# The 64-tap filter of a delta-rule layer as one triangular token block per channel, with new hand-written engine orders

## The reference, cut to what matters

```python
def _dwconv(x, w):                       # w: one filter of K taps for each channel
    K = w.shape[1]
    xt = jnp.pad(jnp.transpose(x, (0, 2, 1)), ((0, 0), (0, 0), (K - 1, 0)))
    y = jax.lax.conv_general_dilated(xt, w[:, None, :], (1,), 'VALID', ..., feature_group_count=w.shape[0])
    return jnp.transpose(y, (0, 2, 1))
...
v = jax.nn.silu(_dwconv(hs @ Wv, conv_v))
o_d, _ = _delta_rule_chunkwise(bh(q), bh(k), bh(v), jnp.transpose(beta, (0, 2, 1)))
paths = jnp.stack([_dwconv(v, fir_s), _dwconv(v, fir_m), _dwconv(v, fir_l), delta_path, v], axis=3)
```

## Time and profile before

| what | value |
|---|---|
| median of 3 executions | 1418.63 us (1417.29 to 1436.04) |
| span of the profiled execution | 1418.5 us |
| TensorE busy | 1334.8 us, 94% |
| weight loads busy | 1166.4 us, 82% |
| DVE busy | 991.1 us, 70% |
| ACT busy | 682.2 us, 48% |
| fill matmuls (L589) | 1024 records, 134.9 us busy |
| filter matmuls (L2337) | 2624 records, 108.6 us busy |
| delta products (L2210) | 3072 records, 103.1 us busy |

### The profile page before, as it was taken

One profiled execution on the slowest core, in us unless ns is written; L12 is line 12 of the kernel. 1 busy time (PEld: TensorE's weight loads), 2 busy tenths in 40 slices (PEclk: granted clock), 3 DMA queues, 4 the chain that ended last, 5 costly groups with the idle time before them and its releaser, 6 DMA issues.

```text
span 1418.5 us, 42978 instructions
## 1 busy us (share of the span) xinstructions
PE 1334.8 (94%) x18644; PEld 1166.4 (82%) x18644; DVE 991.1 (70%) x2959; ACT 682.2 (48%) x1735; POOL 137.9 (10%) x299
## 2 busy tenths in 40 slices
PE   6999998999986899999999999999999999999997
PEld 6788887888643689899789889788979879989976
DVE  7957898678689554667784567796457778455767
ACT  3535763448377456333447533346632444743332
POOL 3111121111110010100110100011010010010000
PEclk9989999999997899999999999999999999999999
DMA  5000000000230200000000000000000000000001
GB/s 160 2 3 2 3 2 2 3 2 3 77 139 19 77 2 1 2 3 2 2 2 1 2 3 3 1 2 1 1 2 4 2 3 1 1 1 3 3 2 31
DMA packets 8509, 20.33 MB, mean 14 GB/s; under 512 B 2304, under 2 KB 6400, under 8 KB 7808
## 3 DMA queue, kind: packets, MB, share of 16 engines
q1 hardware_dynamic: 8320, 17.58, 3.5%
HBM read 16.53 MB, written 1.05 MB: 12 GB/s over the span
## 4 chain that ended last, share of the span: by engine, by line
PE 47%; DVE 12%; ACT 4%; issue 2%; POOL 1%; DVEq 0%
PE PS L2210 6%; PE PS L2337 6%; PE PS L1935 4%; PE PS L1967 3%; PE PS L1956 3%; PE PS L1922 3%; PE PS L2220 3%; PE PS L589 2%; PE PS L690 2%; ACT AR L1985 2%; PE PS L1947 2%; PE PS L2669 1%; PE PS L2678 1%; PE PS L1819 1%; DVE X L2740 1%
## 5 line engine op out<-in xcount | busy, mean ns | idle before, releaser
L589 PE MATMUL PS<-CC 128*128 128x128 f32 x1024 | 134.9, 279 | 0.0
L589 PEld LDWEIGHTS PS<-CC 128*128 128x128 f32 x1024 | 124.5, 193 | 3.1 <-issue 0.5
L1985 ACT ACTIVATE AR<-PS,SC 128x128 f32<-128x128 f32 x256 | 91.1, 378 | 39.3 <-DVE SC L2013 39.3
L2337 PE MATMUL PS<-AR,PA 64*64 64x256 f32 (+43 forms) x2624 | 108.6, 300 | 0.5 <-issue 0.4
L2210 PEld LDWEIGHTS PS<-AR 64*64 64x64 f32 x3072 | 100.5, 135 | 7.2 <-issue 2.2
L2210 PE MATMUL PS<-AR 64*64 64x32 f32 (+1 forms) x3072 | 103.1, 219 | 0.8 <-DVE AR L2463 0.3
L576 POOL TENSOR_SCALAR SC<-mv 128x2 f32<-128x2 f32 x64 | 13.2, 206 | 837.0 <-DVE mv L562 818.4
L2337 PEld LDWEIGHTS PS<-AR,PA 64*64 64x64 f32 x2624 | 85.0, 133 | 6.9 <-issue 2.7
L2010 DVE TENSOR_REDUCE SC<-PS 128x4 f32<-128x512 f32 x64 | 44.2, 691 | 57.1 <-PE PS L1935 56.7
L1935 PE MATMUL PS<-kvt,AR 128*128 128x128 f32 x512 | 68.8, 279 | 2.6 <-ACT AR L1980 2.6
L1935 PEld LDWEIGHTS PS<-kvt,AR 128*128 128x128 f32 x512 | 63.2, 191 | 7.9 <-ACT AR L1980 6.6
(11 more groups left out here) (552 smaller groups left out, 3334.6 us busy)
## 6 DMA issues: line engine op xcount, KB each, us to landing
WC<-in_cw SPq DMA_DIRECT2D x1, 5438.5 KB, 15.8
PA<-in_fd SPq DMA_DIRECT2D x1, 2624.0 KB, 9.3
PA<-in_stat SPq DMA_DIRECT2D x2, 1280.0 KB, 12.0
X<-in_x SPq DMA_DIRECT2D x2, 512.0 KB, 5.5
...
```

What stands on the lines that cost most here:

```text
L589: T.matmul(bank[int(b)][:, 0:P], lhsT=ident, rhs=CC[:, 0:P], start=True, stop=True)
L1985: A.activation(d.blocks[:, h, :], d.bank[:, h * P:(h + 1) * P], ACT.Exp, scale=D2 ** -0.5, bias=d.most[:, h:h + 1], accum_out=d.total[:, h ...
L2337: m = T.matmul(out_[:, :, first:SEQ], lhsT=FD[rows, tap:tap + 64], rhs=d.vp[rows, :, first + 1 - shift:SEQ + 1 - shift], start=starts, sto ...
```

## The change

The 64-tap filter no longer goes by taps. `v` is brought to PSUM a second time, for each sequence with its tokens on 64 partitions and the channels along the free axis (8 more small matmuls, L2260 of the changed kernel), and one ACT instruction puts it into `vs`. For each channel the 64 taps are stored as one 64x64 triangular block. One matmul per channel multiplies it by that channel's tokens in the four sequences: 64x64 weights by 4 columns. That makes 128 matmuls for a unit (L2359), all with output in c = 1. The 3-tap and 15-tap filters go on by taps, 18 taps by two halves, all with output in c = 0 (L2355). Together there are 164 matmuls as before, in 14 groups. A tap is followed by three or four of the channel matmuls. The stored taps keep their size of 82 blocks. The filters wait for `vs` too.

The way back to token partitions has 8 transposes of 64 partitions (L2371) and 4 matmuls (L2373) instead of 4 transposes and 4 matmuls. ACT copies both short filters in one instruction instead of two.

All turn tables of both parts are new. `FILL_A` has 87 digits instead of 139, `FILL_C` 361 instead of 373. In part C the two streams stand further apart: before, both delta layers of a round ran side by side; now that of stream 0 runs beside the cross attention of stream 1, and that of stream 1 beside the end of stream 0's delta layer and what follows. Apart from fill, filter, the 64 matmuls of L2260 and the way back, the matmuls are the same. In its order TensorE goes 80 times from matmuls of one quarter (L2210, L2337) to other shapes or back before, and 144 times after (L2226, L2260, L2355, L2359).

```diff
-        FILL_A = ("011116666666666666666666666666666666666666666666666666000000000000000002222222111111112133333333"
-            "3333330000000000000000111244441300000000000")
+        FILL_A = ("000133337700000000002222222222222111111544462333333333333300001111112221111111111111111")
...
+                self.vs = ar[:, 768:1024].rearrange("p (q n) -> p q n", q=SQ)
...
 
-        def filter_taps():
-
-
-            one = [(0, s) for s in range(3)] + [(2, s) for s in (0, *range(2, 13), *range(13, 64, 2))]
-            two = [(1, s) for s in range(15)] + [(2, s) for s in (1, *range(14, 64, 2))]
-            assert len(one) == len(two) == 41
-            return list(zip(one, two))
+        NTAPS, FGROUPS = 18, 14
+
+        def filter_products():
+
+
+            products = []
+            for n in range(NTAPS):
+                f, shift = (1, n) if n < 15 else (0, n - 15)
+                for r in range(2):
+                    products.append(("tap", r, f, shift))
+                    done = 2 * n + r
+                    products += [("long", o % 2, o // 2, 0) for o in range(P * done // 36, P * (done + 1) // 36)]
+            assert len(products) == 2 * NTAPS + P
+            return products
 
         def tensor_l3_attention(st):
             k, ps, sc, d = "L3a", st.ps, st.sc, Delta(st)
...
             for j in range(TS):
-                m = T.transpose(ps[:, 3, j * P:(j + 1) * P], d.s3[:, 512 + j * P:512 + (j + 1) * P], ident)
+                T.transpose(ps[:, 3, j * P:(j + 1) * P], d.s3[:, 512 + j * P:512 + (j + 1) * P], ident)
+            for q in range(SQ):
+                for rows in d.halves:
+                    m = T.matmul(ps[rows, 3, ST + q * SEQ:ST + (q + 1) * SEQ],
+                                 lhsT=d.s3[rows, 512 + q * SEQ:512 + (q + 1) * SEQ], rhs=cc("ident64")[rows, :],
+                                 start=True, stop=True)
...
-            taps = filter_taps()
-            for n, pair in enumerate(taps):
-                if n == 0:
-                    T.wait_ge(*a.at(f"{k}.v"))
-                    T.wait_ge(*a.at(f"{k}.local"))
-                    T.wait_ge(fd_there, 16)
-                for c, (f, shift) in enumerate(pair):
-                    K, at = FILTERS[f]
-                    o = 0 if f == 2 else ST
-                    starts = shift == (1 if f == 2 and c else 0)
-                    first = 0 if starts else shift
-                    for r, rows in enumerate(d.halves):
-                        out_ = ps[64 * c:64 * c + 64, r, o:o + ST].rearrange("p (q t) -> p q t", q=SQ)
-                        tap = (at + K - 1 - shift) * 64
-                        m = T.matmul(out_[:, :, first:SEQ], lhsT=FD[rows, tap:tap + 64],
-                                     rhs=d.vp[rows, :, first + 1 - shift:SEQ + 1 - shift], start=starts,
-                                     stop=(shift == K - 1 or (f == 2 and shift == K - 2)))
-                if n % 3 == 2 and n < len(taps) - 2:
+            T.wait_ge(*a.at(f"{k}.v"))
+            T.wait_ge(*a.at(f"{k}.v_seqs"))
+            T.wait_ge(*a.at(f"{k}.local"))
+            T.wait_ge(fd_there, 16)
+            todo = filter_products()
+            for n, (kind, r, what, shift) in enumerate(todo):
+                rows = d.halves[r]
+                if kind == "tap":
+                    K, at = FILTERS[what]
+                    tap = (at + K - 1 - shift) * 64
+                    out_ = ps[0:64, r, what * ST:(what + 1) * ST].rearrange("p (q t) -> p q t", q=SQ)
+                    m = T.matmul(out_[:, :, shift:SEQ], lhsT=FD[rows, tap:tap + 64], rhs=d.vp[rows, :, 1:SEQ + 1 - shift],
+                                 start=(shift == 0), stop=(shift == K - 1))
+                else:
+                    o = (NTAPS + what) * 64
+                    m = T.matmul(ps[64:P, r, SQ * what:SQ * what + SQ], lhsT=FD[rows, o:o + 64], rhs=d.vs[rows, :, what],
+                                 start=True, stop=True)
+                if (n + 1) * FGROUPS // len(todo) > n * FGROUPS // len(todo) and n + 1 < len(todo):
                     yield
             m.then_inc(*p.up(f"{k}.fir"))
             yield
             T.wait_ge(*a.at(f"{k}.fir1"))
-            for j in range(TS):
-                for r in range(2):
-                    o = (2 * j + r) * P
-                    T.transpose(ps[:, 0, o:o + P], d.fir[r][:, ST + j * P:ST + (j + 1) * P], ident)
-                    m = T.matmul(ps[:, 1, o // 2:o // 2 + 64], lhsT=d.fir[r][:, j * P:(j + 1) * P],
-                                 rhs=cc("ident64"), start=True, stop=True)
+            for r in range(2):
+                by_seq = d.fir[r][64:P, 0:ST].rearrange("p (i j g) -> p g j i", j=TS, g=2)
+                for f in range(2):
+                    for j in range(TS):
+                        o = (2 * j + f) * P + 64 * r
+                        T.transpose(ps[:, 0, o:o + 64], d.fir[r][0:64, f * ST + j * P:f * ST + (j + 1) * P], ident[0:64, 0:64])
+                    out_ = ps[64 * f:64 * f + 64, 1, 0:ST].rearrange("p (j r i) -> p r j i", j=TS, r=2)
+                    m = T.matmul(out_[:, r, :, :], lhsT=cc("ident64")[64:P, :], rhs=by_seq[:, f, :, :], start=True, stop=True)
...
             A.wait_ge(*p.at(f"{k}.filtered"))
-            for j in range(TS):
-                A.copy(d.paths[:, j, 0:2, :].rearrange("p f (r n) -> p f r n", r=2),
-                       ps[:, 0, j * ST:(j + 1) * ST].rearrange("p (r f n) -> p f r n", r=2, f=2)).then_inc(*a.up())
+            A.copy(d.paths[:, :, 0:2, :], ps[:, 0, :].rearrange("p (j f n) -> p j f n", j=TS, f=2)).then_inc(*a.up())
             A.copy(d.paths[:, :, 2, :], ps[:, 1, 0:ST].rearrange("p (j n) -> p j n", j=TS)).then_inc(
                 *a.up(f"{k}.filtered"))
...
                          scale=0.5).then_inc(*a.up(f"{k}.path_v"))
+            A.activation(d.vs, ps[:, 3, ST:2 * ST].rearrange("p (q n) -> p q n", q=SQ), ACT.Copy, scale=0.5).then_inc(
+                *a.up(f"{k}.v_seqs"))
...
-    fir = np.concatenate([a3["fir_s"], a3["fir_m"], a3["fir_l"]], axis=1)
-    fd = np.zeros((P, fir.shape[1], 64), np.float32)
-    fd[np.arange(P), :, np.arange(P) % 64] = fir
+    fir = np.concatenate([a3["fir_s"], a3["fir_m"]], axis=1)
+    fd = np.zeros((P, fir.shape[1] + 64, 64), np.float32)
+    fd[np.arange(P), 0:fir.shape[1], np.arange(P) % 64] = fir
+    long = a3["fir_l"].reshape(2, 64, 64)
+    for s_ in range(SEQ):
+        for r in range(2):
+            fd[64 * r + s_, fir.shape[1]:, s_:] = long[r][:, ::-1][:, 0:SEQ - s_]
     path = [0, 1, 2, 4, 3]
```

27 lines of the change are left out of this document (12 added, 15 removed), and 295 rows, old and new, of tables (TURNS_A, TURNS_C).

## The result

The changed kernel takes 1447.18 us (median of 4 executions, 1440.37 to 1456.57), the kernel before on the same chip 1422.45 us. The ratio is 1.0163, with a 95% interval of 1.0107 to 1.0218. I had predicted 1394 us, 1369 to 1425: it is slower, where I expected it faster.

What follows compares the result with a forecast made beforehand. TensorE was taken as the bound where delta products and filters stand. Filters -30, tokens +4, switching +7, way back +3, fill -7 and -2 gave -25 us against 1418.5: 1394 us, range 1369 to 1425.

Steps and rivals of the forecast that it cites:

- The clock of part C: Part C: granted clock noted at 0.99 before, no term in the sum; a lower clock considered only for part A's first 60 us.
- The way back: Transposes and matmuls behind the filters: 1.2 to 2.0 us a unit, 3 us more in all (-2 to 5).
- The filters: L2355 and L2359 in part C: 12.1 to 8.3 us a unit, gain 30 us; L2359 records 23 to 29 ns apart.
- the quarters do not pass each other: Rival at L2355 and L2359: second tap records hold up channel records, 14.6 us a unit; 1445 to 1454 us, chance 0.10.
- The columns' slope: Quarter records in the filters: a floor of 60 ns for few columns, otherwise about 0.85 ns for each column.
- Tokens for the channel matmuls: 8 added matmuls a unit, 16 records in two quarters at 29 ns: 0.5 us, 4 us in all; ACT copy free.
- Switching: Changes between quarters and whole array on TensorE: 64 more at 0.11 us each, 7 us added (2 to 8).
- The fill: Fewer fill matmuls: 52 in part A worth 14 us, half taken as 7 us gain; 12 in part C, 2 us.
- The new turns: New order between delta products: TensorE stays the bound, no net gain or loss, with 15 us either way.
- the delta chain bounds: Rival in part C: chain steps wait longer, TensorE idle passes 60 us; 1418 us (1408 to 1426), chance 0.20.

Runs made afterwards that it cites:

- e8: Changed kernel without 112 of the 128 channel matmuls of each unit, way back still alternating (filter result incomplete); 1440.4 us, ratio 1.011.
- e15: Changed kernel with the way back grouped (all 8 transposes, then the 4 matmuls), a repeat of e5; 1390.8 us, 0.975 of the kernel before.
- e1: Changed kernel with 64 moving columns instead of 4 for each channel matmul; 1466.8 us, 1.028 of the kernel before.
- e16: Changed kernel with the way back grouped and 32 moving columns for each channel matmul; 1396.2 us, 0.978 of the kernel before.
- e4: Changed kernel with the old turn tables and fill in part A alone; 1451.0 us, 1.018 of the kernel before.
- e2: Kernel before, old filters kept, with the changed kernel's turn tables and fill in both parts; 1411.2 us, ratio 0.989.
- e5: Changed kernel with the way back grouped: all 8 transposes first, then the 4 matmuls; 1402.3 us, 0.984 of the kernel before.
- e10: e2 with the changed kernel's alternating way back added as unread work behind its own; 1441.9 us, 1.008 of the kernel before.

## Why the prediction was wrong, point by point

Two steps failed. The clock of part C stood in the sum at nothing, as if it had to stay at 0.99, and cost 60 us. The way back stood in it at 3 us and took 12.5. The first alone turned the gain into a loss, and the second, by its alternation, brought the falls of the clock behind it.

**The filters: right in kind, a little too large.** I said 12.1 to 8.3 us for a unit, -30. With low-clock work counted half, they went from 94.8 to 70.1 us: -25, and 25 ns a record in the first group against the 23 to 29 that I named. The rival "the quarters do not pass each other" had the time almost exactly (1445 to 1454) and is false: the order of time shows them passing, and e8 the taps alone at 7.3 us for a unit beside 8.3 predicted for all. A time that fits proves no mechanism. The "strictly in program order" of the Trainium skill that I cited there does not hold between quarters in these traces: in e15, products that stand behind L2375 in the program start at 605.96, before most of its records. The columns' slope was off: 64 of them are no longer at the floor (e1, 41 ns a record instead of 27), 32 are (e16).

**Tokens for the channel matmuls:** +4 predicted, 4.9 measured (16 records in 0.61 us for a unit).

**Switching: mis-sized, and one kind of change missed.** I took 7 us for 64 changes between quarters and whole array. Products (91.6 to 91.9 us, low-clock work counted half) and the cross attention beside them (146.0 to 147.0) grew by 1 us together. But I had counted the way back's transposes and matmuls as one kind of "other shapes", though they are two. The drain that the cited rule speaks of was there, at seven changes inside each way back.

**The way back: mis-sized.** "At 0.14 and 0.22 without any overlap that is 2.0 us" took prices of the earlier trace rows, where transposes and matmuls had one shape of the array, 128 by 128. It took 3.1 to 3.5 us from start to start, the sum 12.5 us more than before and not 3. The 1.2 to 2.0 us that I named came true in e15, at 1.6 to 1.7.

**The fill:** half of 14 us taken in part A; e4 shows none, within its interval of 0.7% to either side. In the first 60 us TensorE's busy time fell by 10.9 us and the part ended 1 us earlier (its successor begins at 384.8, not 385.9). Less fill became idle time and clock 0.86 instead of 1.00, which the next stretch gave back with 1.00 instead of 0.96. In part C the fill's own time fell by 5 us.

**The new turns:** I took 0, "with 15 us either way". e2 measures 16 us of gain (10 to 23 by its interval, fill included), and the holes of part C shrank from 36 to 17 us. The rival "the delta chain bounds" is refuted: it needed over 60 us idle.

**The clock: the step that was not in the sum.** I wrote that part C had 0.99 and left it there, while the edit took the densest records out of the stretch that is mostly quarter work (2624 filter records of up to 256 columns became 576 of those and 2048 of 4) and put an alternating way back behind them. It cost 60 us. It takes both: the new filters with the grouped way back lost 9 us by the clock in e15 and 27 in e5, the old filters with the alternating one had 59 us at the low clock (e10), which is some 20 us of time over e2 and before. My only sentence on a lower clock was about the first 60 us.

The sum again with what was measured, for part C: -25 (filters) + 5 (tokens) + 1 (switching) + 12.5 (way back) - 5 (fill) - 2 (the rest) - 19 (holes) + 60 (clock) = +27, against 27.3. And for the grouped kernel, e15: -23 + 5 + 5 (switching: products 4, cross attention 1) + 0 - 4 - 2 - 19 (holes) + 9 (clock) = -29, which is the difference of its span of 1389.5 to 1418.5. That this lies near my 1394 is partly luck: the holes, which I had at 0, made up for the clock, which I had left out, and for the fill.

## The better version

The changed kernel with the way back grouped beats both, by the two sets of runs 0.984 [0.979, 0.989] and 0.975 [0.971, 0.980] of the kernel before, and 4.0% below the changed kernel on one chip. The filters and the order are worth less apart than together, by ratios from three chips:

| | old order | new order |
|---|---|---|
| old filters | 1 | 0.989 |
| new, way back in twos | 1.040 | 1.016 |
| new, way back grouped | 1.010 | 0.975, 0.984 |

Against the old filters in the new order (0.989 [0.984, 0.993]) the new filters themselves bring 0.5 to 1.4%; they were not run on one chip, and with e5's ratio the intervals touch.
